# Second attention's key and value weights in four transfers per batch pair, and a new written-out order of all five engines

## The reference

```python
x = _L0_xattn_ref(...)  # 8 heads of 32; then U = LN(x) @ W_in.T @ Bmat, and a scan over the 1024 rows:
                        #   s = silu(s @ A.T) + u_t ; x = x + states @ Cmat + mod
x = _L1_xattn_ref(...)  # 16 heads of 64, causal mask: x = softmax(q k^T) v @ wo + bo + x
x = _L2_xattn_ref(...)  # 16 heads of 16, exp * mask: x = LN(attention @ Wo.T + bo + x) * ln_g + ln_b
x = _L3_xattn_ref(...)  # 16 heads of 16, per-batch key mask, then x + fc2(gelu(fc1(LN(x))))
```

## Time and profile before

| what | value |
|---|---|
| median of 3 runs | 1443.99 us (1443.29 to 1445.27) |
| profiled execution, its own time | 1445.13 us |
| its span, first to last instruction | 1443.4 us |
| PE busy | 1362.1 us (94%) |
| DVE busy | 935.7 us (65%) |
| ACT busy | 675.1 us (47%) |
| POOL busy | 559.2 us (39%) |
| mean granted TensorE clock | 0.993 |

### The profile page before, as it was taken

How to read it: one execution, slowest core, us unless ns; L and a number is a source line. 1 busy time by engine, 2 the same in 40 slices (tenths; PEclk the granted TensorE clock), 3 DMA queues, 4 the chain that set the end, 5 groups by cost and what they waited for, 6 DMA issues and landing times.

```text
span 1443.4 us, 22984 instructions
## 1 busy us (share of the span) xinstructions
PE 1362.1 (94%) x8763; PEld 1130.9 (78%) x8763; DVE 935.7 (65%) x2204; ACT 675.1 (47%) x1497; POOL 559.2 (39%) x700
## 2 busy tenths in 40 slices
PE   6999999999899989999999999989998999899989
PEld 4887886767688768878887887868876887698768
DVE  3677764487755776586768466785677567746771
ACT  2566655423455343534454535345434644454344
POOL 4345332013732363345244411283147215620661
PEclk8999999999999999999999999999999999999999
DMA  5043412020000000000000001000000000000000
GB/s 142 23 91 109 137 52 77 1 68 1 1 8 16 8 1 15 9 8 5 5 9 1 23 1 17 16 1 9 22 1 1 9 23 1 0 9 1 1 0 23
DMA packets 46730, 34.10 MB, mean 24 GB/s; under 512 B 21980, under 2 KB 45339, under 8 KB 46107
## 3 DMA queue, kind: packets, MB, share of 16 engines
q1 hardware_dynamic: 45287, 32.43, 8.0%
q10 hardware_dynamic: 1332, 0.17, 0.1%
HBM read 23.26 MB, written 8.39 MB: 22 GB/s over the span
## 4 chain that ended last, share of the span: by engine, by line
PE 75%; DVE 13%; POOL 4%; ACT 4%; issue 2%; DMA 1%; ACTq 1%; DVEq 0%
PE ps L871 9%; PE ps L831 9%; PE ps L881 9%; PE ps L927 8%; PE ps L938 7%; PE ps L850 7%; PE ps L841 5%; PE ps L891 5%; PE ps L797 5%; PE ps L780 4%; DVE zt L1321 3%; PE ps L1032 2%; DVE mx L1346 2%; DVE stat L1308 1%; PE ps L1045 1%
## 5 line engine op out<-in xcount | busy, mean ns | idle before, releaser
L1577 POOL TENSOR_TENSOR rstd<-mv,halfneg 128x1 f32<-128x1 f32 x192 | 109.4, 571 | 490.6 <-DVE mv L1312 489.4
L1158 ACT ACTIVATE pr<-pr 128x616 f32<-128x616 f32 x224 | 159.8, 715 | 177.2 <-DVE pr L1351 89.3
L1616 POOL TENSOR_TENSOR pr<-mx,pr 128x616 f32<-128x616 f32 x128 | 156.5, 1224 | 212.4 <-DVE mx L1346 211.0
L1162 ACT ACTIVATE pr<-ps 128x512 f32<-128x512 f32 x224 | 132.1, 597 | 148.6 <-PE ps L850 148.4
L850 PE MATMUL ps<-ident,pr 128*128 128x128 f32 (+1 forms) x1120 | 160.9, 277 | 8.5 <-POOL pr L1602 4.9
L1410 DVE TENSOR_TENSOR xt<-xt,ps 128x256 f32<-128x256 f32 x192 | 80.0, 416 | 130.6 <-PE ps L891 68.3
L881 PEld LDWEIGHTS ps<-vtab,pr 128*128 128x128 f32 (+1 forms) x1280 | 153.5, 192 | 12.9 <-ACT pr L1162 8.6
L881 PE MATMUL ps<-vtab,pr 128*128 128x102 f32 (+1 forms) x1280 | 161.3, 274 | 1.2 <-ACT pr L1162 1.0
L850 PEld LDWEIGHTS ps<-ident,pr 128*128 128x128 f32 (+1 forms) x1120 | 124.9, 139 | 35.1 <-POOL pr L1602 14.8
L871 PE MATMUL ps<-vwo,pr 128*128 128x256 f32 (+1 forms) x640 | 148.9, 382 | 0.1
L831 PE MATMUL ps<-wk,tt 128*128 128x308 f32 x512 | 145.9, 427 | 1.5 <-DVE xt L1410 1.0
(11 more groups left out here) (200 smaller groups left out, 2414.9 us busy)
## 6 DMA issues: line engine op xcount, KB each, us to landing
out_dram<-xt SPq DMA_DIRECT2D x64, 128.0 KB, 1.7
xt<-in_x_dram SPq DMA_DIRECT2D x32, 128.0 KB, 2.5
xt<-out_dram SPq DMA_DIRECT2D x32, 128.0 KB, 2.1
fc<-in_L_xattn_fc_w_dram SPq DMA_DIRECT2D x2, 1024.0 KB, 5.4
wk<-in_L_xattn_wkv_dram SPq DMA_DIRECT2D x1, 2048.0 KB, 8.1
front<-in_L_xattn_wkv_dram SPq DMA_DIRECT2D x1, 2048.0 KB, 7.7
wo<-in_L_xattn_wo_dram SPq DMA_DIRECT2D x1, 1024.0 KB, 5.4
kb<-in_L_xattn_wq_dram SPq DMA_DIRECT2D x1, 1024.0 KB, 6.6
```

The source lines that it names most:

```text
L1158: ac(v, v, ACT.Exp, scale=-ATTN[key[0]].scale).then_inc(done["expo"], 1)
L1162: ac(pr[:, run.lane, 0:4 * P], bank(run.lane, 0), ACT.Copy).then_inc(done["pturn_main"], 1)
L1577: p.tensor_tensor(rstd[:, n:n + 1], mv[:, n, 1:2], halfneg[:, :], ALU.pow).then_inc(done["rstd"], 1)
L1616: p.tensor_tensor(p8, mx[:, run.lane, :].unsqueeze(2).to_broadcast([P, HG, KEYS]), p8, ALU.subtract).then_inc(done["below"], 1)
```

## The change

`wkv1_get` becomes four steps for each pair, each of which fetches 512 of the 2048 columns; the reader waits for all four. Every string of `TURNS` is replaced. All steps, their operations, tiles and sizes stay as they are.

```diff
+WKV_PARTS = 4
...
-    steps = [] if pair else ([("v0_put", p)] + [("weights_get", i) for i in range(LOADS - 1)] + [("wkv1_get", p), ("masks", "2"), ("weights_get", LOADS - 1)])
+    wkv1 = [("wkv1_get", p + str(i)) for i in range(WKV_PARTS)]
+    steps = [] if pair else ([("v0_put", p)] + [("weights_get", i) for i in range(LOADS - 1)] + wkv1 + [("masks", "2"), ("weights_get", LOADS - 1)])
...
 TURNS = {
     "tensor": (
-        "iiiiiiiiiiii1i0iiiiiiii0iiii0ii123120203102301021310123020110323103102102020121330031021302112310212320310321021"
+        "iiiiiiii0ii1i0iiii11i0iiii01i0iii0iii120312012103102130201321302310213023102303120123013012012310232032103032012"
...
             def wkv1_get(key, run):
-                if key == "0":
+                pair, part = map(int, key)
+                n = 2 * L1.width // WKV_PARTS
+                cols = slice(part * n, (part + 1) * n)
+                if pair == 0:
...
-                sp.dma_start(wkv1[int(key)], by_rows("L1_xattn_wkv")).then_inc(wkv1_in, 16)
+                sp.dma_start(wkv1[pair][:, :, cols], by_rows("L1_xattn_wkv")[:, :, cols]).then_inc(wkv1_in, 16)
...
                     if a is L1:
-                        pe.wait_ge(wkv1_in, 16 * (pair + 1))
+                        pe.wait_ge(wkv1_in, 16 * WKV_PARTS * (pair + 1))
```

More of the change, by code:

```diff
@@ L134, in table_steps @@
     else:
-        steps += [("wkv1_get", p)]
+        steps += wkv1
     steps += [("vtw_zero", p)]
@@ L239 @@
[L239 to L248, removed]
@@ new lines @@
+        "0012320310321321023101210320310312230102320310321321102312120320213023230130013210210313120203210312320320120301"
+        "3032102313210213021321023132032013310321302102310321123013123203231023130121323021323012a3a23aasaaaasaasasasasas"
+        "asasasaasaasaasaasaasaasaasaasasaasasasaasasasaasaasasaasaasasaaaaasaaaaasaaa0aa23s01011232030102121320303010120"
+        "1212312020310313123020201011313230202012131030302321201010230232103101201020130231320110132132130103012210210323"
+        "0120131012130330210313201020303132102013202123030310312120210130102323201200101032130321302110131132013120231013"
@@ new lines @@
+    "scalar": (
+        "iiiiii0ii101ii10ii0iii1ii021203123021003113201013203120223133020012131032013201302220010323321030121130131202322"
+        "0100323321031211032102322130210200313302031311203212201302002133302130321113202213013233210300231013112032122313"
+        "302132323100123aa23saasasasasasasaassaasaasaasaasaaaasaaasaasaasasaasssssssssssssss01023102132031020130211023201"
+        "2133020130121320023110303212010202313102010233121013302103120120130130123102011320301032123002123003231120301120"
+        "3212013001323210110233120311230201213003121032201333210232031032121302203131320021313002210132130020321112032031"
+        "03132120320130103221210310323102032103132120031212030131230203103121203203103212bb1323bbbbbb2332bb2bb323bbbb2302"
+        "2031031302102321030312023121023131230203103121203023031102211323020130132201003231132100232103123210231030103212"
+        "0312023112330201301321200321310301212030320121331020210312310320212302133102301230301220132102313123020310312120"
+        "3023101302121003230121313020201331210203221301332102023103013212031023121303202301312102302331010221313020231310"
+        "2120303032131213322"),
@@ new lines @@
+    "gpsimd": (
+        "ii01iii2132300010111022230330101211302230320020313a1a12012020320331311122220303031013121220230303101312212203303"
+        "3011012232333120123301a2b011023320100121220301313200020101131302222112033323102033110322101332120001130013100000"
+        "2011121213031322100323222210333103321321302001213132032011300001110112230213302213302220211230233033132132201300"
+        "1132003312100001111100122203313220313021222233332332320023113230320012112020331312000203013110122212333123203132"
+        "0311002231123033200011212203013132000201113130022121232330321330211300213320123230001121230203131200020311131002"
+        "22122133303213302130102211332203300101102023231310002020313110122212333130223312031132230"),
@@ L288 @@
     "sync": (
-        "10230123aaaaaaaaa00a11a22a3a30a0a121aa2aa0303a1a1aaa202a303a1a1a2a2a0a303a1a1a2a2003311220331200a30111223323baa0"
-        "0112233001122330123000111bb223323001122330011223301130223"),
+        "01230123aaaaaa0a10aa12aa23a0a30a1a1aaaa203203a1a1aaa202a303a1a1a2a2a0a3a0a3a1a1a2a2a030311223031200a01312213323b"
+        "bbbaa00112233001122330123000111bb223332001122330011223302130231"),
 }
```

67 lines of the change are left out of this document (28 added, 39 removed).

## The result

| what | before | after |
|---|---|---|
| median, same chip | 1443.64 us | 1383.48 us (1380.49 to 1386.6) |
| ratio to before | 1 | 0.9584 (95% interval 0.9569 to 0.9598) |
| profiled execution, its span | 1443.4 us | 1384.4 us (its own time 1386.1) |
| sum of the norm's groups | 117.0 us | 85.1 us |
| PE idle (span less busy) | 81.3 us | 41.6 us |

The change makes the kernel 60.2 us faster. The forecast was 14 us, 1430 us in a range of 1411 to 1444: the sign was right, the size was not, and the result lies outside the range. The four runs with the change fall into two pairs, 1380.5 and 1380.9 us at a mean granted clock of 0.996 and 1386.1 and 1386.6 us at 0.991, so a difference of some 6 us between versions of the new order isn't told by its time alone. Lines of the engine code are 5 higher than in the kernel before.

What follows compares the result with a forecast made beforehand. The prediction saw PE, busy 1362.1 of 1443.4 us, with many short waits for DVE and ACT; 5.5 + 7.1 + 1.9 = 14.5 us off gave a forecast of 1430 us, range 1411 to 1444 us.

Steps and rivals of the forecast that it cites:

- step 3: Set-up transfers: splitting the 2 MB `wkv` fetch lets the `load` behind it land earlier, removing PE's wait of 1.9 us.
- Step 1: Norms on DVE held by POOL: fewer other-lane steps behind `rstd` return 14.9 us of DVE, 5.5 us on the path.
- Step 2: PE's list: fewer steps right behind the step they need, so shorter waits for DVE and ACT; net 7.1 us, bounds 0 and 16.2.
- path share of 0.37: The norm line's 43 us in the chain out of its 117 us of work, applied to the 14.9 us returned.
- larger gain: Rival: all covers count in full, 33.0 us, giving 1411 us; gaps inside PE's busy time could close too; chance 0.18.
- The waits only change places: Rival: crowded stretches come from amount of work, not order; only the transfer's 1.9 us stay, 1442 us; chance 0.10.
- crowded stretches: Six stretches of 36 us, DVE and POOL each busy 26 to 28 us on average, holding 30 us of idle PE.
- slower rival: POOL stands still behind its own waits for norms, 16 us of POOL; 1458 us, or 1447 with a third on path; chance 0.10.
- signs of being wrong: Norm line stays at 117 us, or falls with PE idle still 81 us, or a new wait over 2 us before `k_mm`.

Runs made afterwards that it cites:

- the kernel with nearly the same counts: Kernel before, POOL's list alone: at 37 places the norm's own follower moved directly behind its `rstd`, past another lane's `prebias` or `keep`; 1442.88 us, ratio 0.9995.
- the kernel with the rewritten lists: Kernel before, PE's list kept; phase 1 lists of DVE, ACT and POOL rewritten to follow the last PE step ahead in each lane; 1970.6 us, ratio 1.3643.

## Why the prediction was wrong in size

Beside step 3, two things of the forecast failed. Its counts of neighbours in the lists, on which steps 1 and 2 rest, did not give the size of what came back, and it put the gaps inside PE's busy time at nothing. It took 14.5 us off the idle time of PE; measured are 39.7 us off the idle and 19.3 off the busy time.

**Step 3, the transfer (1.9 us): failed.** Four pieces in a row delay the `load` more than one did (7.61 against 7.08 us), and the order with a single fetch has the whole gain. The wait of 1.93 us is gone, but by the order, not by the pieces, though these do shorten the landing where other transfers stand between them (2.6 us against 6.3). The fetch itself was covered as forecast; no wait stands before `k_mm`.

**Step 1, held norms (5.5 us): mechanism right, size wrong twice.** "If the excess goes with the count" gave 102 us for the groups; measured were 85.1. The counts of neighbours are not the cause: the kernel with nearly the same counts has 107.1 us. An order doesn't tell whether POOL's next step is ready when the `rstd` ends, and only another lane's step that starts then holds the norm: with 33 long steps instead of 38 behind an `rstd`, 3 norms instead of 23 were held there. And the path share of 0.37 is an average over two kinds: the norms behind long steps gave back 11.4 us for 19.7 us of excess, those behind row steps 5.4 us for 18.1. The port's part came to some 17 to 19 us, about three tenths of the gain, above even the bound of 14.9 set for this step.

**Step 2, PE's pairs (7.1 us): not borne out as a cause.** The waits fell further than forecast, from 25.8 to 8.6 us (4.4 + 2.0 for `heads`, none for the residual, 1.6 + 0.6 for ACT), but pulling such pairs apart alone costs 55 us. The fewer pairs went together with the better order; that they made any of it is not shown.

**What the sum missed.** Of the gain, 41 us are there without any held norm, and the sum had 9 for them (steps 2 and 3). What the runs show of them: the gain is spread over the set-up, phase 0 and phase 1, it is gone when PE's new list is set against other partners, and single exchanges on PE cost a microsecond each. That makes it likely, not shown, that the 41 us lie in how the five lists fit each other. The views that bounded them were there: PE's idle 81 us, and a chain with a quarter of its length off PE. That half of this idle time could come back was never priced; the "larger gain" rival named the gaps inside PE's busy time, gave them no number, and stopped at the waits that could be tied to counted neighbours. Which placements carry the 41 us stays open.

**The rivals.** The larger gain, 1411 us, had the direction and was too small as well. "The waits only change places" fell, though its premise held: DVE and POOL are as busy in the crowded stretches as before. The slower rival is a real mechanism, 13 us when POOL's list alone is changed at 67 places. The change escapes it: PE's wait for `maskmul` fell from 4.9 to 3.0 us. That it does so because the other lists moved with POOL's is argued, not shown.

**The signs named ahead.** PE's idle time 66 us (measured 41.6), its busy time at or below 1362 (1342.8), the `load` within 5 us (2.6), the crowded stretches as busy (they are): all point the right way; the idle time and the norm's groups went well beyond. The `load`'s sign came true and was worth nothing. None of the signs of being wrong came up: they told the sign of the change, not its size.

## What to carry to other kernels

When all orders of a tightly scheduled kernel are replaced at once, don't price the change by counting neighbours: bound it by PE's idle time, the share of the chain that is not PE's and the gaps inside PE's busy time, and give a large part of that a chance. In such a kernel an edit to one engine's list alone mostly costs time (here about 1 us for each exchange on PE), and even one that takes 10 us off an engine may return nothing. A norm held by POOL is worth freeing where POOL's blocking step is long (here 0.30 us each, against 0.08 behind short ones), and whether it is held is read from the durations in the trace, not from the order. Where the two engines fight, a dearer form of the instruction that the other engine doesn't hold up can win, if it computes the same (here it was used to measure only).

## What the runs showed of the hardware

- The accumulator form of the norm was never held by POOL: 489 to 542 ns, plus a read of 83 ns, where the plain form takes 415 ns in the middle and 1466 at most. The Trainium skill (SBUF — State Buffer, "Who interferes with whom") states that this form of `tensor_scalar` does not take the shared pair; the rows here agree. The dearer form made the kernel before 13.5 us faster; the read overlapped the step behind it, and DVE's busy time fell by 12 us.
- With PE idle for 431 of 1970 us, the kernel with the rewritten lists has a mean granted clock of 0.889, against 0.993 before, so part of its time is PE at the lower of its two levels (1.2 and 2.4 GHz). Its busy time is 1539.7 us for the same 8763 products that took 1362.1: long waits cost more than the time waited.
- A `load` that is issued behind a fetch of `wkv` on the same queue landed 0.32 to 0.35 us after it in all four kernels looked at: behind the whole fetch before the change and in the new order, behind the last of four pieces in a row, and behind the first piece in the changed kernel. Its own landing time, 2.6 to 7.6 us, followed from when that fetch landed.
